# Moving two kinds of store from ScalarE's DMA queue to SyncE's in a one-core attention and mixture-of-experts kernel

## The chip, the core and the metric

The kernel runs on one core of a Trainium2 chip. The number that counts is the device time of one execution in microseconds (us). Five engines work in parallel, each through its own instruction stream in a fixed order: TensorE (PE, with its weight loads PEld), VectorE (DVE), ScalarE (ACT), GpSimd (POOL) and SyncE (SP), which only starts transfers (DMA). ACT and POOL can start transfers too; in the profile these issues stand as SPq, ACTq and POOLq. Engines wait for each other and for transfers through semaphores.

## What is computed

Sixteen sequences of 512 rows by 256 columns go through one layer: attention with 16 heads of 16 columns, rotary positions and a linear position bias, then a residual and a layer norm; then a shared feed-forward part plus the best two of eight experts for each row, then again residual and norm. Cut to what matters:

```
qkv = x @ qkv_w.T;  q, k = rotary(q), rotary(k)
w = softmax(q @ k.T * SCALE + min(j - i, 0) * slope * 8)
x = layernorm(x + (w @ v) @ proj_w.T + proj_b)
shared = silu(x @ sW1 + sb1) @ sW2 + sb2
top_vals, top_idx = top_k(sqrt(softplus(x @ routing_W.T + bias)), 2)
y_e = silu(x @ rW1[e] + rb1[e]) @ rW2[e] + rb2[e]
x = layernorm(x + shared + sum over the two experts of top_val * y_e)
```

## The kernel before

**Steps.** All engines run the same loop over steps `s` (from -36 to 711), and a table of numbers says in which step each job of each sequence falls. A sequence takes 32 steps of attention (steps 0 to 511 for the sixteen), in four groups of eight; its later jobs follow at fixed distances. A step is no barrier: it only fixes the order inside each engine's stream. Semaphores do the rest, so an engine can be ahead of another or behind it.

**Attention, seen from SP.** In every eight steps, for one group of four heads, SP does the following in this order: it writes row maxima to memory (`m_out`, L452) and reads them back into the operand `qa` (`m_rows_in`, four transfers at L459); it writes the sums of the softmax (`sums_out`, L464), waits until they have landed and reads them back in another shape (`sums_in`, L470); it loads the next group's operands (`assemble`, six transfers at L390 and L393, four at L429 and L430); it writes the reciprocals (`rec_out`, L474), waits for the landing and spreads them (`rec_rows`, four at L484). Beside these it writes projected queries and keys (`parts_out`, L422).

**Sparse experts.** Fourteen of the sequences go through a sorted layout: their rows are scattered to memory by expert, in three groups of 6, 6 and 2 sequences, and are then worked off in blocks of 256 rows, 31, 31 and 15 of them (77). `BLOCKS_AT` gives their steps: in the first group mostly one block in four steps, in the second one in two, in the third one in each step. For a block, SP reads two table entries into registers (L499, L500) and loads the rows `xg` (L503), the weights `wb` (L507) and a bias (L510), two steps ahead of its first use or, where blocks are dense, one; PE turns the rows (L802), multiplies by the first weights (L810) and the second (L818, L820); ACT copies the result to `yb[q % 3]` (`down_block`, L1472), three steps after the turn; and one step later the copy is stored to `d_y` (`store_block`, L1479) from ACT's stream, just behind that step's two exponentials (L1368). ACT's copy of block q + 3 waits until that store has landed.

**Finals.** When a group's blocks are stored, POOL gathers each row's two expert results (L1602), DVE adds them to the base (L1192, L1194), which SP has loaded into `bs[b % 2]` (`base_in`, L527, which waits on the landing of the result that was in that buffer, L526), POOL computes the scale, and ACT normalizes in place (`norm2`, four at L1420, step offset `NORM2` = 8). One step later ACT's stream stores the result to `out` (L1532, offset `OUT` = 9).

**Dense experts.** The last two sequences go through all eight experts. SP loads each expert's weights (`load_expert`, L520 and L521); the buffers are four, and a load waits until the expert four earlier is through. PE multiplies at L832 and L845.

Of the kernel before, what the change touches and what calls it, by code (L numbers as in the profile page):

```python
# [67 lines left out]
LOADB, TURNB, UPB, GATEB, DOWNB, STOREB = (-2, 0, 1, 2, 3, 4)  # L68
# [9 lines left out]
DENSE_AT = ((93, 1), (86, 1))  # L78
LOADD, GATED, DOWND = (-5, 1, 2)
WEIGHTS, VAR3, NORM3, OUTD = (0, 24, 25, 27)  # L80
BASE_IN, GATHER, ADD, VAR2, NORM2, OUT = (-1, (1, 2, 2, 4), (3, 4, 5, 6), 6, 8, 9)
LATE, PREP, PADS = 11, (18, 20, 22, 24), 40

WARM = (5, 6, 4, 4, 5)
# [6 lines left out]
ROWS = 256  # L91
# [5 lines left out]
FIRST_BLOCK = [sum(NBLOCKS[:g]) for g in range(len(GROUPS) + 1)]  # L97
# [43 lines left out]
def block_due(s, at):  # L141

    return BLOCK_OF.get(s - at, -1)


def final_due(s, at):

    return FINAL_OF.get(s - at, -1)
# [32 lines left out]
def _build(nc, ctx, A, out):  # L181
# [95 lines left out]
    yb = [sb(f"yb{i}", [128, 2, C]) for i in range(3)]  # L277
# [4 lines left out]
    bs = [sb(f"bs{i}", [128, 4, C]) for i in range(2)]  # L282
# [44 lines left out]
    out_w = [sem(f"out_w{i}") for i in range(2)]  # L327
# [38 lines left out]
    def bk(job, i, b):  # L366

        return G[(job, i), b][0]

    def full(job, i, b):  # L370

        return G[(job, i), b][1] + 1
# [25 lines left out]
    def _(e):  # L398
# [93 lines left out]
        def load_block(q):  # L492
            g = GROUP_OF_BLOCK[q]
            j = q - FIRST_BLOCK[g]
            if j == 0:
                e.wait_ge(s_tab, g + 1)
                e.wait_ge(rows_w, 16 * 8 * (LAST_OF[g] + 1))
                e.wait_ge(pad_w, 32)
            row = e.value_load(tab[0:1, g, j:j + 1], min_val=0, max_val=E * REGION - ROWS)  # L499
            wrow = e.value_load(tab[0:1, g, JMAX + j:JMAX + j + 1], min_val=0, max_val=(E - 1) * 128)  # L500
            if q >= NX:
                e.wait_ge(g_full[bk("turnb", 0, q - NX)], full("turnb", 0, q - NX))
            e.dma_start(xg[q % NX][:, :, :], d_x[g % 2][bass.ds(row, ROWS), :].rearrange("(p k) c -> p k c", k=2)  # L503
                        ).then_inc(xg_in[q % NX], 16)
            if q > 3:
                e.wait_ge(g_full[bk("downb", 0, q - 4)], full("downb", 0, q - 4))
            e.dma_start(wb[q % 4][:, :], A["wb"][bass.ds(wrow, 128), :]).then_inc(wb_in[q % 4], 16)  # L507
            if q == 0:
                e.wait_ge(rb_w, 32)
            e.dma_start(rb2[q % 4][0:2, :], d_rb[bass.ds(wrow, 2), :]).then_inc(wb_in[q % 4], 16)  # L510

        def load_expert(n):
# [7 lines left out]
            e.dma_start(wbd[n % 4], A["wb"][x * 128:x * 128 + 128, 0:512]).then_inc(wbd_in[n % 4], 16)  # L520
            e.dma_start(rbd[n % 4][0:2, :], d_rb[x * 128:x * 128 + 2, :]).then_inc(wbd_in[n % 4], 16)  # L521

        def base_in(b):
            e.wait_ge(base_w, 16 * (b + 1))
            if b > 1:
                e.wait_ge(out_w[b % 2], 16 * (b // 2))  # L526
            e.dma_start(bs[b % 2][:, :, :], d_base[b].rearrange("(t p) c -> p t c", p=128)).then_inc(bs_in[b % 2], 16)  # L527
# [14 lines left out]
        for s in range(FIRST, LAST):  # L542
            if (g := (s - M_OUT) // 8 - 1) >= 0 and (s - M_OUT) % 8 == 0 and g < 4 * NB:
                m_out(g)
            if (g := (s - M_IN) // 8 - 1) >= 0 and (s - M_IN) % 8 == 0 and g < 4 * NB:
                m_rows_in(g)
            for g in range(4):
                if (b := due(s, EVAC + SUMS_OUT + 8 * g)) >= 0:
                    sums_out(4 * b + g)
                if (b := due(s, EVAC + SUMS_IN + 8 * g)) >= 0:  # L550
                    sums_in(4 * b + g)
                if (b := due(s, EVAC + REC_OUT + 8 * g)) >= 0:
                    rec_out(4 * b + g)
                if (b := due(s, EVAC + REC_IN + 8 * g)) >= 0:
                    rec_rows(4 * b + g)
            if s == 3:
                load_xT(1)
            if s == LATE:
                e.dma_start(idf[:, :], A["k_idf"]).then_inc(l_id, 16)
                load_x(0)  # L560
                e.dma_start(wp[:, :, :], A["wp"]).then_inc(l_w, 16)
                e.dma_start(pb[:, :], A["pb"].rearrange("(a c) -> a c", a=1).broadcast_to([128, C])).then_inc(l_w, 16)
                e.dma_start(w1[:, :, :], A["w1"]).then_inc(l_w, 16)
                e.dma_start(w2[:, :], A["w2"]).then_inc(l_w, 16)
                e.dma_start(rw[:, :, :], A["rwT"]).then_inc(l_w, 16)
                e.dma_start(b1[:, :], A["b1"]).then_inc(l_w, 16)
                e.dma_start(bias2[0][E:E + 1, :], A["sb2"].rearrange("(a c) -> a c", a=1)).then_inc(l_w, 16)
                for t in range(4):
                    e.dma_start(ebb[:, t, :], A["eb"].rearrange("(a c) -> a c", a=1).broadcast_to([128, E])).then_inc(l_w, 16)
                e.dma_start(bias2[0][0:E, :], A["rb2"]).then_inc(l_w, 16)  # L570
                e.dma_start(wkey[:, :, :], A["k_key"]).then_inc(l_w, 16)
                e.dma_start(before[:, :, :], A["k_before"]).then_inc(l_w, 16)
                e.dma_start(run0[:, :], A["k_run"]).then_inc(l_w, 16)
                e.dma_start(tk[:, :], A["k_tk"]).then_inc(l_w, 16)
                e.dma_start(th[:, 0:128], A["k_on2"]).then_inc(l_w, 16)
                e.dma_start(bd[:, :], A["b1s"]).then_inc(l_bd, 16)
            if s == PREP[3]:
                e.wait_ge(s_rb, 2)
                e.wait_ge(s_zero, 1)
                for k in range(2):  # L580
                    e.dma_start(d_rb.rearrange("(x r) c -> r x c", r=128)[k], bias2[1 + k]).then_inc(rb_w, 16)
                e.wait_ge(rb_w, 32)
                e.dma_start(sb2[0:2, :], d_rb[E * 128:E * 128 + 2, :]).then_inc(rb_in, 16)
            if s == PADS:
                for i in range(2):
                    e.dma_start(d_x[i].rearrange("(x r) c -> r x c", x=E)[0:ROWS],
                                A["x"][0, 0:ROWS].rearrange("r (x c) -> r x c", x=1).broadcast_to([ROWS, E, C])
                                ).then_inc(pad_w, 16)
            for q in LOAD_BLOCKS.get(s, ()):
                load_block(q)  # L590
            for i in range(4):
                if (b := due(s, QK[i][-1] + SHUFFLE[i] + PARTS_OUT)) >= 0:
                    parts_out(b, i)
                    if 4 * b + i == 1:
                        e.wait_ge(p_k0, 16)
                        key_rows(0)
            if (g := (s - ASSEMBLE) // 8) >= 0 and (s - ASSEMBLE) % 8 == 0 and g < 4 * NB:
                assemble(g)
            if (b := due(s, XT_LOAD)) > 1:
                load_xT(b)  # L600
            if (b := due(s, X_LOAD)) > 0:
                load_x(b)
            if 0 <= (b := due(s, BASE_OUT)) < SPARSE:
                base_out(b)
            for n in LOAD_EXPERTS.get(s, ()):
                load_expert(n)
            if (k := last_due(s, OUTD)) >= 0:
                e.wait_ge(s_od, k + 1)
                e.dma_start(out[SPARSE + k].rearrange("(t p) c -> p t c", p=128), x1[(SPARSE + k) % 2][:, :, :]
                            ).then_inc(out_d, 16)  # L610
            if (b := final_due(s, BASE_IN)) >= 0:
                base_in(b)
        for i in range(2):
            e.wait_ge(out_w[i], 16 * ((SPARSE + 1 - i) // 2))
        e.wait_ge(out_d, 16 * DENSE)
# [741 lines left out]
    def _(e):  # L1357
# [114 lines left out]
            e.mul(yb[q % 3][:, :, :].rearrange("p k c -> p (k c)"), pG[bk("downb", 0, q)][:, :], 0.5  # L1472
                  ).then_inc(g_free[bk("downb", 0, q)], 1)

        def store_block(q):
            g = GROUP_OF_BLOCK[q]
            j = q - FIRST_BLOCK[g]
            e.wait_ge(g_free[bk("downb", 0, q)], full("downb", 0, q))
            e.dma_start(d_y[g][j * ROWS:(j + 1) * ROWS, :].rearrange("(p k) c -> p k c", k=2), yb[q % 3][:, :, :]  # L1479
                        ).then_inc(y_w[q % 3], 16)  # L1480

        e.dma_start(sl[:, :], A["slopes"].rearrange("(a h) -> a h", a=1).broadcast_to([128, H])).then_inc(l_sl, 16)
        e.dma_start(hot, A["k_hot"]).then_inc(l_pos, 16)
        e.dma_start(bpos[0:32], A["k_pos"][0:32]).then_inc(l_pos, 16)
# [4 lines left out]
        for s in range(FIRST, LAST):  # L1489
            if 0 <= s - LAG < NC:  # L1490
                exps(s - LAG)
            if (q := block_due(s, STOREB)) >= 0:
                store_block(q)
            for g in range(4):
                if (b := due(s, EVAC + 8 * g)) >= 0:
                    evacuate(4 * b + g)
# [30 lines left out]
                e.activation(sp[:, 2, 0:8 * ALL_GROUPS[g]], sp[:, 1, 0:8 * ALL_GROUPS[g]], ACT.Exp).then_inc(s_u, 1)  # L1527
            if (b := final_due(s, NORM2)) >= 0:
                norm2(b)
            if (b := final_due(s, OUT)) >= 0:  # L1530
                e.wait_ge(s_o, b + 1)
                e.dma_start(out[b].rearrange("(t p) c -> p t c", p=128), bs[b % 2][:, :, :]).then_inc(out_w[b % 2], 16)  # L1532
            if (b := due(s, UP[1])) >= 0:
                up(b)
            if (n := dense_due(s, 0)) >= 0:
# [192 lines left out]
```

## Time and profile before

| What | us |
|---|---|
| median of three runs | 1660.75 |
| the three runs | 1657.20, 1660.75, 1663.59 |
| the profiled execution, its own time | 1663.59 |
| its span in the trace | 1661.8 |
| transfers' mean rate from 1300 to 1400 | 206 GB/s |

PE is busy for 88% of the span, DVE 71%, ACT 61%, POOL 44%. ACT's figure counts its computing instructions; register, semaphore and DMA-issuing instructions of an engine are not counted as busy, so SP has no figure at all although its stream has some two thousand instructions. What SP does is seen in the timeline, in the list of what it waited for, and in the chain: the work that ended last, followed back from the end, at each step to what released it. SPq in that chain is time in which nothing but SP's issuing stood between one event and the next.

### The profile page before, as it was taken

The page shows a single profiled execution, that of the slowest core. Times are in us where ns is not written, and L with a number is a line of the kernel's source. Part 1 is how long each engine was busy: PE and PEld are TensorE (multiplying, and loading weights), DVE is VectorE, ACT ScalarE, POOL GpSimd, SP SyncE. Part 2 cuts the span into 40 slices and gives each one's busy share as a digit, 9 for nine tenths or more (in the row PEclk, how much of TensorE's full clock was granted, in tenths as well). Part 3 has the DMA queues.
Part 4 walks back from the last instruction along what each step waited for, and adds up shares of the span by engine and source line. Part 5 has one row for each costly group of instructions (what it writes and reads, how often), then busy time and mean ns, then how long its engine had stood idle before and what let it go on. Part 6 is the DMA issues. An engine that isn't in the chain of part 4 may idle for free.

```text
span 1661.8 us, 33130 instructions
## 1 busy us (share of the span) xinstructions
PE 1458.4 (88%) x11110; PEld 801.2 (48%) x11110; DVE 1171.7 (71%) x2631; ACT 1019.3 (61%) x1742; POOL 723.9 (44%) x655
## 2 busy tenths in 40 slices
PE   7987999999999889899999899988888999896467
PEld 4433444444444435555555544454455555564345
DVE  7665777878778787666666677857776577645674
ACT  1465666666767656666677576666566587675242
POOL 2233353635545343541535253533666344255630
PEclk8789899999999989999999999999999899998789
DMA  7334243434343324454545433443566566686531
GB/s 208 115 109 147 91 124 101 129 108 132 102 123 116 115 92 141 132 175 139 178 138 165 130 120 116 128 139 120 166 214 222 177 217 209 192 257 212 168 106 51
DMA packets 185349, 242.00 MB, mean 146 GB/s; under 512 B 67239, under 2 KB 104190, under 8 KB 185182
## 3 DMA queue, kind: packets, MB, share of 16 engines
q1 hardware_dynamic: 154746, 181.18, 36.4%
q0 software_dynamic: 10752, 29.37, 5.4%
q10 hardware_dynamic: 19684, 29.33, 5.0%
q8 instruction: 91, 1.49, 0.4%
q14 instruction: 76, 0.62, 0.1%
HBM read 152.53 MB, written 91.44 MB: 147 GB/s over the span
## 4 chain that ended last, share of the span: by engine, by line
PE 51%; DVE 15%; SPq 14%; DMA 10%; issue 6%; POOL 2%; ACT 2%; POOLq 0%; ACTq 0%; DVEq 0%
PE pS L641 15%; PE pV L683 9%; PE pG L707 6%; DVE negm L932 5%; PE pG L729 3%; PE pG L716 3%; SPq L390 2%; DMA xg<-d_x 2%; PE pS L647 2%; DMA d_rec<-scr 2%; PE pG L810 2%; SPq L459 2%; PE pG L818 2%; SPq L499 1%; DMA d_sum<-pvs 1%
## 5 line engine op out<-in xcount | busy, mean ns | idle before, releaser
L932 DVE TENSOR_REDUCE negm<-pS 128x1 f32<-128x512 f32 x1024 | 659.6, 683 | 336.4 <-PE pS L647 329.6
L1368 ACT ACTIVATE ee<-pT,slp 128x512 f32<-128x512 f32 x1024 | 649.0, 684 | 216.8 <-PE pT L668 215.2
L641 PE MATMUL pS<-ka,qa 62*128 62x512 f32 x1024 | 485.4, 509 | 81.0 <-DVE negm L932 68.3
L662 PE MATMUL pT<-qa,ka 64*128 64x512 f32 x1024 | 480.9, 504 | 0.2 <-ACT ee L1368 0.2
L641 PEld LDWEIGHTS pS<-ka,qa 62*128 62x128 f32 x1024 | 198.4, 194 | 330.0 <-issue 312.8
L683 PE MATMUL pV<-ee,vv 128*32 128x512 f32 (+1 forms) x2048 | 286.8, 633 | 0.0
L647 PE MATMUL pS<-mAB,tri 64*128 64x64 bf16 x2048 | 243.6, 200 | 0.0
L668 PE MATMUL pT<-mAB,tri 64*128 64x64 bf16 x2048 | 239.9, 198 | 0.0
L1555 POOL TENSOR_TENSOR raw<-raw,rope 128x512 f32<-128x512 f32 x61 | 78.2, 1282 | 330.0 <-DVE sh L966 329.9
L662 PEld LDWEIGHTS pT<-qa,ka 64*128 64x128 f32 x1024 | 195.6, 191 | 4.5 <-issue 3.1
L647 PEld LDWEIGHTS pS<-mAB,tri 64*128 64x128 bf16 x2048 | 119.8, 99 | 139.6 <-issue 107.3
L1575 POOL TENSOR_TENSOR rs<-ve,minus 128x4 f32<-128x4 f32 x32 | 34.1, 1067 | 280.3 <-DVE ve L1014 280.3
L707 PE MATMUL pG<-xT,wqkv 128*128 128x512 f32 x256 | 149.6, 670 | 4.6 <-DVE wqkv L1274 2.4
L1602 POOL DMA_INDIRECT gg<-d_y,posy x112 | 111.5, 995 | 60.1 <-issue 29.0
L1590 POOL DMA_INDIRECT d_x<-x,pos x112 | 115.3, 1030 | 48.0 <-issue 24.6
L668 PEld LDWEIGHTS pT<-mAB,tri 64*128 64x128 bf16 x2048 | 118.0, 97 | 28.2 <-issue 24.8
L1609 POOL TENSOR_TENSOR pvs<-pvs 128x512 f32<-128x512 f32 x32 | 40.7, 1271 | 172.8 <-DVE pvs L956 172.8
L729 PE MATMUL pG<-wp,pvs 128*128 128x256 f32 x256 | 70.3, 409 | 28.9 <-POOL pvs L1609 28.9
L818 PE MATMUL pG<-wb,zbb 128*128 128x256 f32 x308 | 93.6, 397 | 1.0 <-DVE zbb L1182 1.0
L1384 ACT COPY raw<-pG 128x512 f32<-128x512 f32 x63 | 36.9, 586 | 85.6 <-PE pG L707 68.3
L810 PE MATMUL pG<-xgT,wb 128*128 128x256 f32 x308 | 84.1, 397 | 4.0 <-DVE x L1178 3.2
L1456 ACT COPY xgT<-pG 128x512 f32<-128x512 f32 x77 | 44.8, 582 | 66.4 <-PE pG L802 66.4
(186 smaller groups left out, 2192.8 us busy)
## 6 DMA issues: line engine op xcount, KB each, us to landing
d_part<-parts SPq DMA_DIRECT2D x63, 512.0 KB, 2.8
qa<-d_part SPq DMA_DIRECT2D x378, 64.0 KB
wb<-in_wb SPq DMA_DIRECT2D x77, 256.5 KB
xg<-d_x SPq DMA_DIRECT2D x77, 256.0 KB, 2.9
d_y<-yb ACTq DMA_DIRECT2D x77, 256.0 KB, 2.6
ka<-d_part SPq DMA_DIRECT2D x128, 128.0 KB
xT<-in_xT SPq DMA_DIRECT2D x16, 512.0 KB
ka<-d_part SPq DMA_DIRECT2D x128, 64.0 KB
```

The source lines that it names most:

```text
L641: e.matmul(pS[:, k, :], qa[g % 4][r, i, t * 128:t * 128 + 128].bitcast(F32R), ka[g % 4][r, i, :].bitcast(F32R), start=True, stop=False)
L647: last = e.matmul(pS[:, k, c0:c0 + 64], tri[r, a, :], mAB[r, 1, i, :], start=False, stop=(a == 1))
L662: e.matmul(pT[:, k, :], ka[g % 4][r, i, kt * 128:kt * 128 + 128].bitcast(F32R), qa[g % 4][r, i, :].bitcast(F32R), start=True, stop=False)
L668: last = e.matmul(pT[:, k, c0:c0 + 64], tri[r, 2 + a, :], mAB[r, 0, i, :], start=False, stop=(a == 1))
L683: last = e.matmul(pV[32 * hh:32 * hh + m, :], vv[b % 2][:, 17 * kt + r0:17 * kt + r0 + m, h], ee[:, k, (4 * w + 2 * (hh % 2) + hh // 2) % ...
L707: last = e.matmul(pG[bk("qk", i, b)][:, :], wqkv[:, c, col:col + 128], xT[b % 2][:, c, :], start=(c == 0), stop=(c == 1))
L729: last = e.matmul(pG[bk("proj", j, b)][:, t * C:(t + 1) * C], pvs[:, (4 * b + 2 * p) % SETS, (2 * j + t) * 128:(2 * j + t + 1) * 128], wp[ ...
L810: last = e.matmul(p[:, 0:ROWS], wb[q % 4][:, c * 128:c * 128 + 128], xgT[q % 2][:, c, :], start=(c == 0), stop=(c == 1))
L818: e.matmul(p[:, k * C:(k + 1) * C], zbb[q % 2][:, k * 128:k * 128 + 128], wb[q % 4][:, 256:512], start=True, stop=False)
L932: e.tensor_reduce(negm[:, g % 2, j, t + k:t + k + 1], pS[:, k, :], AX, ALU.max, negate=True).then_inc(s_max, 1)
L1368: e.activation(ee[:, k, d % 7, :], pT[:, k, :], ACT.Exp, scale=slp[:, 6, h:h + 1]).then_inc(s_exp, 1)
L1590: e.indirect_dma_start(d_x[g % 2], bass.IndirectOffsetOnAxis(pos[:, b % 2, n, t:t + 1], 0), x1[b % 2][:, t, :], None).then_inc(rows_w, 16)
```

## The change

`store_block` and the store of the normalized result move from ACT's stream to SP's. In a step, SP now issues the block's store behind the loads of blocks that fall in that step and ahead of `parts_out` and `assemble`; the result's store is the last thing of its step. Each brings its wait along: the store of a block waits on ACT's copy, that of a result on `norm2`. `OUT` goes from 9 to 8, so that the result's store stands in the step of `norm2` itself.

```diff
-BASE_IN, GATHER, ADD, VAR2, NORM2, OUT = (-1, (1, 2, 2, 4), (3, 4, 5, 6), 6, 8, 9)
+BASE_IN, GATHER, ADD, VAR2, NORM2, OUT = (-1, (1, 2, 2, 4), (3, 4, 5, 6), 6, 8, 8)
@@ SP's stream
+        def store_block(q):
+            g = GROUP_OF_BLOCK[q]
+            j = q - FIRST_BLOCK[g]
+            e.wait_ge(g_free[bk("downb", 0, q)], full("downb", 0, q))
+            e.dma_start(d_y[g][j * ROWS:(j + 1) * ROWS, :].rearrange("(p k) c -> p k c", k=2), yb[q % 3][:, :, :]
+                        ).then_inc(y_w[q % 3], 16)
...
             for q in LOAD_BLOCKS.get(s, ()):
                 load_block(q)
+            if (q := block_due(s, STOREB)) >= 0:
+                store_block(q)
...
             if (b := final_due(s, BASE_IN)) >= 0:
                 base_in(b)
+            if (b := final_due(s, OUT)) >= 0:
+                e.wait_ge(s_o, b + 1)
+                e.dma_start(out[b].rearrange("(t p) c -> p t c", p=128), bs[b % 2][:, :, :]).then_inc(out_w[b % 2], 16)
@@ ACT's stream: store_block is gone, and with it
-            if (q := block_due(s, STOREB)) >= 0:
-                store_block(q)
...
-            if (b := final_due(s, OUT)) >= 0:
-                e.wait_ge(s_o, b + 1)
-                e.dma_start(out[b].rearrange("(t p) c -> p t c", p=128), bs[b % 2][:, :, :]).then_inc(out_w[b % 2], 16)
```

In the order of the instructions, SP's stream gets 91 transfers more (77 blocks, 14 results). Two places matter.

The first is SP in the second group of blocks, in one eight-step round; the difference shows both kinds of store around `rec_out`. `d_rec` holds the reciprocals, `rb_0` is a block's bias, `yb` its result, `bs` a normalized sequence; line numbers behind the change are seven or more higher for the same code.

```order
 L510 ISA
 L510 DMA rb_0<-d_rb 2x256
-L474 DMA d_rec<-scr 128x16 [waits s_rec]
+L527 DMA d_y<-yb 128x512 [waits g_free0]
+L474 DMA d_rec<-scr 128x16 [waits s_rec]
+L624 DMA out<-bs 128x4x256 [waits s_o]
 L484 DMA rb<-d_rec 16x512 [waits s_att,rec_w1]
 L484 DMA rb<-d_rec 16x512 x3
```

A block's store now stands between the last load of the block and the next thing of the round, here `rec_out`; the result's store stands between `rec_out` and the wait for its landing.

The second is SP near the end, where `rope` and `wqkv` are reused as buffers for the dense experts' weights and `parts` for their biases. Before:

```order
L521 DMA parts<-d_rb 2x256
L527 DMA bs<-d_base 128x4x256 [waits out_w1,base_w]
L520 DMA rope<-in_wb 128x512 [waits s_yd]
L521 DMA parts<-d_rb 2x256
L520 DMA rope<-in_wb 128x512 [waits s_yd]
```

Now:

```order
L521 DMA parts<-d_rb 2x256
L534 DMA bs<-d_base 128x4x256 [waits out_w1,base_w]
L624 DMA out<-bs 128x4x256 [waits s_o] x2
L520 DMA rope<-in_wb 128x512 [waits s_yd]
L521 DMA parts<-d_rb 2x256
```

The stores of the last two sparse sequences, with their waits on `norm2`, now stand ahead of the weight loads of the last sequence's first four experts.

## Rows read from the trace of the kernel before

**Rows 1.** The page, part 4: the chain by engine.

```profile
PE 51%; DVE 15%; SPq 14%; DMA 10%; issue 6%; POOL 2%; ACT 2%; POOLq 0%; ACTq 0%; DVEq 0%
```

**Rows 2.** What PE waited for, 640 to 1515: total, times, longest.

```profile
PE pG L802 <- DMA xg<-d_x: 38.7, 21, 4.0
...
```

**Rows 3.** What SP waited for, 1214.2 to 1276.7: total, times, longest.

```profile
SPq L484 <- DMA d_rec<-scr: 7.0, 2, 3.7
SPq L470 <- DMA d_sum<-pvs: 2.7, 2, 1.6
```

**Rows 4.** The same, 1341.4 to 1403.3.

```profile
SPq L470 <- DMA d_sum<-pvs: 5.2, 2, 2.9
SPq L484 <- DMA d_rec<-scr: 4.5, 2, 2.7
```

**Rows 5.** The same, 1276.8 to 1341.4.

```profile
...
SPq L474 <- DVE scr L952: 4.5, 1, 4.5
...
```

**Rows 6.** SP's first table load per block, 1203.6 to 1283.4 and 1329.7 to 1414.1.

```profile
L499 SPq TENSOR_LOAD <-tab x11: 451/473/1201, 1203.7 to 1281.6; - x11
...
L499 SPq TENSOR_LOAD <-tab x11: 453/474/967, 1331.6 to 1412.5; - x11
```

**Rows 7.** The chain where the first stretch ends: start, length, what.

```profile
1283.36 2.87 DMA xg<-d_x
...
```

**Rows 8.** The chain on SP, 1273: start, length, what.

```profile
1273.11 0.29 SPq L510
...
1273.51 0.35 SPq L422
...
1273.91 0.73 SPq L459
```

**Rows 9.** Timeline of ACT, 1236: start, length, engine, line, operation.

```profile
1236.25 0.67 ACT L1368 ACTIVATE ee<-pT,slp 128x512 f32<-128x512 f32 x1
1236.36 0.33 ACTq L1479 DMA_DIRECT2D d_y<-yb  x1
1236.82 0.68 ACT L1368 ACTIVATE ee<-pT,slp 128x512 f32<-128x512 f32 x1
...
1239.74 1.26 ACT L1368 ACTIVATE ee<-pT,slp 128x512 f32<-128x512 f32 x2
```

**Rows 10.** The moved stores, all: issue in ns min/median/max; landing in us.

```profile
L1479 ACTq DMA_DIRECT2D d_y<-yb x77: 326/326/355, 643.6 to 1521.7; - x77
...
DMA to landing us min/median/max: 2.0/2.6/6.0
...
L1532 ACTq DMA_DIRECT2D out<-bs x14: 378/396/462, 1203.2 to 1610.4; - x14
```

**Rows 11.** ACT's first store and SP's bias load at the same place of the order.

```profile
L1479 ACTq DMA_DIRECT2D d_y<-yb x11: 326/326/333, 1206.1 to 1282.6; - x11
...
1210.30 0.29 SPq L510 DMA_DIRECT2D rb<-d_rb  x1
```

**Rows 12.** What SP waited for, 831.9 to 855.2.

```profile
...
SPq L474 <- DVE scr L952: 0.9, 1, 0.9
...
```

**Rows 13.** What SP waited for, 1444 to 1503.

```profile
...
SPq L474 <- DVE scr L952: 1.9, 2, 1.2
...
SPq L507 <- PE pG L820: 1.3, 1, 1.3
```

**Rows 14.** A window near the end: busy PE, PEld, DVE, ACT, POOL; clock, DMA share, GB/s.

```profile
1614.70:1620.40 5.70, 5.69 (x11) 3.27 (x12) 2.27 (x10) 2.07 (x4) 2.53 (x3) 0.50 0.00 0
```

**Rows 15.** Timelines near the end, of SP, PE and ACT.

```profile
1587.62 0.33 SPq L520 DMA_DIRECT2D rope<-in_wb  x1
...
1600.67 1.88 PE L832 MATMUL pG<-x1T,rope 128*128 128x512 f32 x4
1614.71 1.19 PE L791 MATMUL pG<-w,hs 128*128 128x256 f32 x2 [12.17 <-DVE hs L1164]
...
1610.40 0.38 ACTq L1532 DMA_DIRECT2D out<-bs  x1
```

More of the change, by code:

```diff
@@ L1473, in down_block @@
                   ).then_inc(g_free[bk("downb", 0, q)], 1)
[L1475 to L1480, printed above, removed]
         e.dma_start(sl[:, :], A["slopes"].rearrange("(a h) -> a h", a=1).broadcast_to([128, H])).then_inc(l_sl, 16)
```

## The prediction, made before the run

> **What bounds the kernel now.** I read the chain of waits first. It runs on PE for half the span, but 14% of it is SP's issuing and 10% are transfers, and ACT's issuing has 0% [rows 1]. Then what PE waits for while blocks are worked off, from 640 to 1515: most often and longest for the block rows `xg` that SP loads, 38.7 us in 21 waits, more than for DVE [rows 2]. Then what SP itself waits for. From 1214 to 1277 and from 1341 to 1403 it waits for nothing but the landing of its own two small round trips, the sums and the reciprocals [rows 3, 4]; there is no wait for an engine. There SP is the bottleneck: whatever is put into its stream pushes back all that stands behind it. The chain says the same: it lies on SP and on SP's transfers without a break from the table load at 1203.7 to the load that lands for PE behind 1283.36, and again from about 1330, just ahead of the table load at 1331.6, to the load that follows the last table load at 1412.5 [rows 6, 7]. Between the two SP does wait for DVE, 4.5 us [rows 5]. In the first group of blocks it is less tight: in the round from 831.9 to 855.2 its longest engine wait is 0.9 us [rows 12]. In the third group, 1444 to 1503, they are 1.9 and 1.3 us in two and a half rounds [rows 13].
>
> **What ACT gets back: about nothing.** A block's store sits behind the first exponential of its step. At 1236.36 it is issued in 0.33 us while that exponential is still running (1236.25 to 1236.92), and the second begins 0.57 us behind the first; of the two from 1239.74, with no store between, the second begins 1.26 - 0.69 = 0.57 us behind the first as well [rows 9]. So 77 times 0.33 us [rows 10] are hidden under ACT's arithmetic, and taking them away saves 0. One result store near the end is not hidden: at 1610.40 it stands 0.38 us between the last `norm2` and an exponential for which DVE waits [rows 15]. Gain: 0.4 us.
>
> **What SP pays.** The nearest row is `parts_out`, one transfer with one wait. The bias load ends at 1273.40, `parts_out` is issued in 0.35 us, and the next transfer starts at 1273.91 [rows 8]: 0.51 us in all, of which some 0.07 would stand there as a gap anyway. I take 0.44 for a block's store, and 0.48 for a result's, whose issue is 0.07 longer on ACT (0.396 to 0.326) [rows 10]; all together 77 × 0.44 + 14 × 0.48 = 40.6 us of SP's time. From below the cost is 0, where SP would have waited anyway; from above it is these 40.6. Does the new wait on ACT's copy block SP? No: SP lags. Counting through the new order, the second group's first store within the stretch falls behind the bias load that ends at 1210.6, and ACT had issued that store at 1206.1 [rows 11]. Laid on each other in this way, the two streams show SP at the place of the store mostly 2 to 14 us after the copy is finished. So the stores go out late but without waiting. Late stores hold ACT's copy three blocks on; in the third group, one block per step, I find 2 us or more between the landing (2.6 us) and that copy, so this costs nothing in the forecast.
>
> Group by group:
> - Second group, the two stretches on SP: 11 loads in each [rows 6]. The first load has a result's store behind it and no block's, the last load ends the stretch. That leaves 9 and 10 block stores and 4 result stores, of which one stands between `rec_out` and the wait for its landing and is hidden. 19 × 0.44 + 3 × 0.48 = 9.8 us, all on the path.
> - Between the stretches: 6 block stores and a result, 3.1 us, against 4.5 us of waiting for DVE [rows 5], some of which come behind a late load. I take 1.0; from 1414 to 1444, 0.5 of four stores' 1.8.
> - Third group, 13 block and 2 result stores until 1503: 6.7 us against 3.2 us of engine waits [rows 13]. 2.5 us, between 0 and 6.7.
> - First group, 31 stores, two in a round, 0.88 us a round. PE waits for `xg` in about every second round. There the store ahead of `assemble` counts, and often that behind `rec_rows`: 8 rounds × 0.66 = 5.3, and 0.2 for the others; 5.5, between 0 and 31 × 0.44 = 13.6. The round in rows 12 has 0.9 us of slack for its 0.88, which is why I don't take more.
> - The end: the weight load for the last sequence's first expert is issued at 1587.62 and used by PE at 1600.67, in time that PE has to spare [rows 15]. Now it stands behind two result stores, the second of which waits for the `norm2` that ends at 1610.37. Issues at 1610.45 and 1610.9, landing about 2.9 us later (the time of a block's rows, of the same size [rows 7]): 1613.8. PE then starts 0.9 us sooner than its 1614.71, but with the four products that it had done before, 1.88 us at the higher clock. PE had idled for 12.17 us [rows 15], and its granted clock was 0.50, the lower level (1.2 GHz), from 1614.7 to 1620.4 [rows 14]. If that stretch starts at 1613.8 and is as long, 3.6 us of it go to these products, 2.1 to the next, and the dense stage starts 0.6 us later. Bounds: -0.4 if the load lands sooner, +3.5 if it takes the 6.0 us of the slowest block store [rows 10]. With the 0.4 of ACT: +0.2 us.
> - In the tail before that, SP is held by a result's store ahead of the last reciprocals' rows. They arrive a little later, while POOL is still busy with gathers: 0.
>
> Sum: 9.8 + 1.0 + 0.5 + 2.5 + 5.5 + 0.2 = 19.5 us on the profiled execution's 1663.6, which is 1683.1. The median of the runs is 2.8 us below that execution, so I forecast 1680.3, rounded to 1680; from the bounds of its terms this case reaches from 1670 to 1691.
>
> The Trainium skill ("DMA: Bandwidth & Descriptors", section "Issuing engines are not separate DMA queues") says that transfers started by different engines run on the same DMA engines, and that spreading them saves only the sequencer's time to issue, usually small beside the transfer. Beside the landing of 2.6 us the 0.33 us is small indeed [rows 10]; but by that rule the sequencer's time is all that this change gives up, and it gives it up on the one that has none to spare.
>
> **Rivals.**
> - *Absorbed.* SP's round has waits on landings; if the loads that become late are ones for which PE has slack in more rounds than I think, only the two bound stretches count, and of them perhaps half: about 5 us, 1666. For it: 4.5 us of slack lie between the stretches [rows 5]. Against it: no engine wait at all inside them [rows 3, 4]. Chance 0.17.
> - *Queued behind the store.* Now 256 KB of a block's store go ahead of the reciprocals' small transfer on SP's own queue, and SP stands still until that has landed. At the mean rate from 1300 to 1400, 206 GB/s, 256 KB are 1.3 us; in eight rounds of the second and third group that adds 10 us: 1691. For it: that landing cost 3.7 us where loads stood just ahead [rows 3]. Against it: the same bytes passed the same engines before. Chance 0.16. The Trainium skill ("DMA: Bandwidth & Descriptors", section "Queues, rings and completion order") has each DMA engine take one queue's descriptors in ring order and alternate between queues by packets. By that rule the small transfer would overtake a store on ACT's queue but not one on SP's, which speaks for this rival; no row of before can show it.
> - *SP seizes up.* A late store holds ACT's copy in the third group, PE waits for ACT, and the weights for the last experts land late (+3.5): 15 blocks × 0.7 us more, 1680 + 10.5 + 3.3 = 1694. The 2 us of room speak against it. Chance 0.07.
> - *Faster.* ACT's issues were not hidden, and their 77 × 0.33 + 14 × 0.40 = 31.0 us come off the path: 1660.75 - 31.0 + 19.5 = 1649. It wins from the point where more than 19.5 of the 31.0 us stood on the path. ACT has 2% of the chain and its issuing 0% [rows 1], and rows 9 show one overlapped. Chance 0.05.
>
> **How the numbers follow.** Forecast 0.55, then 0.17, 0.16, 0.07 and 0.05. What a measurement can tell from no change is about 0.5%, 8.3 us: up to 1669.1 counts as the same. Slower: 0.55 + 0.16 + 0.07, less 0.01 for the low edge of my own case, 0.77. Same: 0.17. With the 0.01 and part of the faster case that stays small, 0.18. Faster: 0.05. The range of 8 in 10 reaches from 1663, which holds most of the absorbed case, to 1697, which takes in the landings' case and the stall.
>
> **What would show it.** Right: in the second group SP's engine waits near 0, PE's waits for `xg` longer in sum than 38.7 by some 10 to 20 us; block issues of 0.35 us on SP with no wait before them; exponentials still 0.57 us apart on ACT, so ACT's busy time unchanged and its idle time larger; PE's first product of the last sequence at about 1614 plus the shift. The landings' rival would show as longer waits of L484 on `d_rec`. I am wrong if PE's waits for `xg` don't grow, if SP's new stores wait for ACT's copies, or if the stretches around 1203 to 1283 and 1330 to 1414 keep their length.

## The result and the profile after

| | median us | runs | ratio to before, 95% interval |
|---|---|---|---|
| before, same chip | 1661.93 (1657.2 to 1663.59) | 4 | |
| changed | 1680.96 (1677.53 to 1693.48) | 4 | 1.0133 [1.0097, 1.0168] |

The change costs 1.33%, 22.1 us by the ratio, with an interval of 16 to 28 us; between the two medians lie 19.0. 1680 was forecast, and slower. The record holds nine more runs of the changed kernel, from 1678.16 to 1695.45 us; the median of all thirteen is 1683.03. The profiled execution of the changed kernel is the slowest of them, 1695.45 us, 14.5 above the median in the table, so what it shows of sizes by stage is too large by that much in all; the sizes below are taken from ratios. In the changed kernel the block's store is L527 and the result's L624; lines of SP between them are 7 higher, those of PE, DVE and ACT mostly 12 higher. In the tables of this document two of e8's six runs (4198.71 and 7189.06 us) and one run of the kernel before beside e4, e5, e6 and e8 (2142.97 us) were in a slow state and count in no ratio.

The page's chain by engine, which answers to [rows 1]:

```profile
PE 44%; SPq 21%; DVE 13%; DMA 11%; issue 7%; another core or an unknown queue 1%; POOL 1%; ACT 1%; POOLq 0%; DVEq 0%; ACTq 0%
```

SP's issuing has 21% of the chain, where it had 14%. What PE waited for from 640 to 1530, against [rows 2] (total, times, longest):

```profile
PE pG L814 <- DMA xg<-d_x: 50.6, 23, 5.9
...
```

PE's waits for SP's loads grew by 11.9 us, as the prediction asked for. The moved stores on SP, against [rows 10] (issue in ns: min/median/max):

```profile
L527 SPq DMA_DIRECT2D d_y<-yb x77: 3/353/1452, 645.8 to 1552.6; - x77
...
L624 SPq DMA_DIRECT2D out<-bs x14: 378/416/562, 1211.9 to 1640.8; - x14
```

What SP waited for in the two stretches that answer to [rows 3] and [rows 4], from 1220.0 to 1292.9 and from 1360.5 to 1424.8:

```profile
SPq L484 <- DMA d_rec<-scr: 4.6, 1, 4.6
SPq L470 <- DMA d_sum<-pvs: 2.6, 2, 1.5
SPq L390 <- PE pT L680: 0.4, 1, 0.4
```

```profile
SPq L470 <- DMA d_sum<-pvs: 3.6, 2, 2.5
SPq L484 <- DMA d_rec<-scr: 2.0, 1, 2.0
```

Still no wait of SP for an engine but 0.4 us; it never waits there for ACT's copy. In the whole run the list has 0.9 us of that wait, once.

The list's waits for the reciprocals' landing (L484) look shorter than before, 4.6 and 2.0 us after 7.0 and 4.5, but it names one wait in each stretch where SP makes two such round trips. SP's timeline has them all; in the first stretch:

```profile
1236.49 0.42 SPq L474 DMA_DIRECT2D d_rec<-scr  x1
1241.71 1.72 SPq L484 DMA_DIRECT2D rb<-d_rec  x4
...
1273.04 0.46 SPq L474 DMA_DIRECT2D d_rec<-scr  x1
1276.47 1.72 SPq L484 DMA_DIRECT2D rb<-d_rec  x4
```

From the issue of `rec_out` to that of its rows pass 5.22 and 3.43 us here, 3.05 and 3.95 in the second stretch, 15.7 in all. The same four trips take 3.64, 4.22, 2.28 and 3.12 before, 13.3 in all. With 256 KB of a block's store just ahead of each of them in SP's own ring they are longer by 0.6 us each on average, in one execution. Whether that comes from the bytes is taken up with e3.

A row of SP's timeline (start, length, engine, line) shows a store in its place, between the bias load and the query rows, 0.47 us from its start to that of the next transfer:

```profile
1259.76 0.29 SPq L510 DMA_DIRECT2D rb<-d_rb  x1
1260.10 0.35 SPq L527 DMA_DIRECT2D d_y<-yb  x1
1260.57 1.26 SPq L390 DMA_DIRECT2D qa<-d_part  x2
```

On ACT, against [rows 9], a pair of exponentials that had the store behind its first:

```profile
1253.93 1.25 ACT L1380 ACTIVATE ee<-pT,slp 128x512 f32<-128x512 f32 x2
```

1.25 us for two of 0.68, so the second begins 0.57 us behind the first, as with the store between them. ACT got nothing back there, and its busy time over the whole run is 1021.4 us after 1019.3.

### The profile page after: what moved, and what is told of

Read it like the earlier page. It is cut to its first block, busy times and chain, and to the rows that moved or that the text cites. A ratio compares the mean times of both kernels' runs of the same rounds, so it can differ in the third digit from the quotient of the medians.

```text
span 1693.6 us, 33130 instructions
## 1 busy us (share of the span) xinstructions
PE 1470.3 (87%) x11110; PEld 807.4 (48%) x11110; DVE 1169.2 (69%) x2631; ACT 1021.4 (60%) x1742; POOL 723.3 (43%) x655
## 4 chain that ended last, share of the span: by engine, by line
PE 44%; SPq 21%; DVE 13%; DMA 11%; issue 7%; another core or an unknown queue 1%; POOL 1%; ACT 1%; POOLq 0%; DVEq 0%; ACTq 0%
PE pS L653 13%; PE pV L695 8%; DVE negm L944 5%; PE pG L719 5%; SPq L390 3%; SPq L459 3%; DMA xg<-d_x 3%; PE pG L728 3%; DMA d_rec<-scr 2%; PE pG L741 2%; PE pS L659 2%; SPq L499 2%; SPq L393 2%; SPq L484 2%; SPq L430 1%
## 5 line engine op out<-in xcount | busy, mean ns | idle before, releaser
L1609 POOL TENSOR_TENSOR pvs<-pvs 128x512 f32<-128x512 f32 x32 | 40.7, 1273 | 177.1 <-DVE pvs L968 177.1
L814 PE MATMUL pG<-idf,xg 128*128 128x128 f32 x308 | 50.2, 287 | 51.5 <-DMA xg<-d_x 50.6
```

## The experiments

Each ratio is to runs of the kernel before on the same chip, taken beside those of the experiment. That kernel's median was 1663.76 us beside the first four experiments of the table, 1675.14 beside the next four, 1660.75 and 1673.55 beside the last two pairs, so plain times of different groups are not compared; a difference in us is the ratio's excess times that median.

| experiment | ratio, 95% interval | us |
|---|---|---|
| e1: only the block stores on SP | 1.0115 [1.0070, 1.0161] | +19.1 |
| e2: only the result stores on SP | 1.0034 [1.0005, 1.0063] | +5.7 |
| e3: 77 small transfers added on SP | 1.0124 [1.0077, 1.0171] | +20.6 |
| e7: changed, block stores in SP's waits | 1.0012 [0.9983, 1.0042] | +2.0 |
| e4: 154 small transfers added on SP | 1.0257 [1.0203, 1.0311] | +43.1 |
| e5: before, key rows' loads on ACT | 0.9848 [0.9795, 0.9901] | -25.5 |
| e6: changed, key rows' loads on ACT | 0.9928 [0.9901, 0.9955] | -12.1 |
| e8: e7 and key rows' loads on ACT | 0.9860 [0.9798, 0.9921] | -23.5 |
| e9: block stores of the first group on SP | 1.0031 [1.0009, 1.0052] | +5.1 |
| e10: block stores of the later groups on SP | 1.0077 [1.0049, 1.0104] | +12.8 |
| e11: 77 small transfers added on ACT | 0.9996 [0.9970, 1.0021] | -0.7 |
| e12: e2 with `norm2` a step earlier | 1.0023 [0.9994, 1.0053] | +3.8 |

### Which stores cost: blocks alone, results alone

e1 is the change without L624 and with `OUT` left at 9; e2 is the change without L527, its block stores on ACT as before.

> Only the 77 block stores are on SP; the 14 result stores stay on ACT at offset 9. Theory (SP's issue time on the path): the 19.5 us of the forecast less the three result stores in the bound stretches (1.4) and the late weight load at the end (0.6, with the 0.4 us of ACT not regained): about 17 us over before, 1679. Rival (the result stores, whose wait on norm2 blocks SP, carry the loss): at most 5 us over before, 1667.

> Only the 14 result stores are on SP, at offset 8; the block stores stay on ACT. Theory: 3 x 0.48 us in the bound stretches and 0.2 at the end, about 2 us over before, 1664, which is near what can't be told from no change. Rival (result stores carry the loss): 12 us or more over before, 1674.

The blocks cost 19.1 us, as the theory had it. The results cost 5.7, more than the 2 expected, though the interval reaches from 0.8 to 10.5. The trace of e2, an execution 13.3 us above its median, suggests a cause that the forecast had ruled out for block stores and taken over for results without a count. What SP waited for in e2 from 1282.5 to 1320.7:

```profile
SPq L470 <- DMA d_sum<-pvs: 5.2, 1, 5.2
SPq L615 <- ACT bs L1423: 3.9, 1, 3.9
...
```

SP stands at the result's store 3.9 us for ACT's `norm2`, with all its loads behind it, and 2.3 us in the next such round: where SP is not held up by 77 block stores it reaches these waits early enough to stand in them.

e12 puts `norm2` where SP no longer meets it; against e2:

```diff
-BASE_IN, GATHER, ADD, VAR2, NORM2, OUT = (-1, (1, 2, 2, 4), (3, 4, 5, 6), 6, 8, 8)
+BASE_IN, GATHER, ADD, VAR2, NORM2, OUT = (-1, (1, 2, 2, 4), (3, 4, 5, 6), 6, 7, 8)
```

> Only the result stores on SP, as in the kernel that cost 5.6 us instead of the 2 expected, but with ACT's norm2, on which each store waits, one step earlier (step 7 of the sequence's last phase instead of 8), so that it is over before SP comes to the store. Theory (of the 5.6 us some 6 were SP's waits of 3.9 and 2.3 us for norm2 within the second group): these waits go, ratio 1.000 to 1.002. Rival (the price is the 14 issues or where the stores land): ratio 1.003 to 1.005 as before. Where norm2 in its new place waits for DVE and holds ACT, the time rises though the waits go, and the pair decides nothing.

The two waits are gone from the second group in its trace, and the ratio is 1.0023, between what the two sides expected and with an interval that holds both. Whether the waits or the 14 issues make up the price of the results alone stays open.

### Issue time or bytes

e3 leaves all stores on ACT and adds, at each place where the change issues a block's store, a transfer of 4 KB with the same wait; e4 adds two.

```diff
+        def tiny(q):
+            e.wait_ge(g_free[bk("downb", 0, q)], full("downb", 0, q))
...
+            e.dma_start(d_small[q], idf[:, 0:8]).then_inc(small_w, 16)
...
+            if (q := block_due(s, STOREB)) >= 0:
+                tiny(q)
```

> The kernel before, with its block stores on ACT, and in addition at each of the 77 places where the changed kernel has a block store on SP a transfer of 4 KB over 128 partitions (instead of 256 KB) with the same wait; its data are not used. It costs SP the same issue but puts no bytes into its queue. Theory (issue time): the same loss as with the block stores alone, about 17 us over before, 1679. Rival (the bytes that go ahead of SP's small transfers in its own queue): at most 7 us over before, 1669.

> The kernel before, with two extra transfers of 4 KB on SP at each place where the change issues a block store (154 in all, one wait per place as before). With one extra transfer per place the time rose from 1663.8 to 1684.3, 20.6 us or 0.27 us for each of 77. Theory (SP's issue time is what costs, and it adds up): the second transfer costs at least as much as the first, +40 to +50 us, 1704 to 1714. Rival (the first transfer costs only by its place or by its wait on ACT's copy, the work that follows is free): not above 1690, as with one. Rival (SP has slack in part of the program, so that more load makes further rounds bound): the second costs more than the first, above 1714.

4 KB cost 20.6 us, 256 KB cost 19.1 (e1): the bytes do not carry the loss, and the rival by which e3 costs at most 7 us has fallen, since its interval begins at 12.8. Nor do the bytes show in the four round trips of the reciprocals above: by the timelines they take 17.8 us in e1 and 17.4 in e3, and 14.8 in e11, where SP's stream is that of before (13.3). An effect of the bytes of a few us in all is not excluded: e1 and e3 each have an interval of some 15 us. Two transfers cost 43.1 us, within the 40 to 50 expected: 2.1 times one, 0.28 us for each of 154. The added ones on SP in e4 (issue in ns, min/median/max):

```profile
L529 SPq DMA_DIRECT2D d_small<-idf x77: 12/353/643, 649.4 to 1566.6; - x77
L530 SPq DMA_DIRECT2D d_small<-idf x77: 3/432/1895, 649.8 to 1567.0; - x77
```

### The same transfers on ACT

e11 adds the same 77 transfers of 4 KB behind ACT's block stores, without a wait of their own.

```diff
             if (q := block_due(s, STOREB)) >= 0:
                 store_block(q)
+                tiny(q)
```

> The kernel before, with 77 extra transfers of 4 KB issued by ACT, each right behind a block store (so two issues stand behind the first exponential of the step). The same 77 on SP cost 20.6 us. Theory (ACT's issues are hidden under the exponential in front of them): ratio 0.998 to 1.003, and the second exponential still starts about 0.57 us behind the first. Rival (the second issue sticks out of the 0.67 us of the exponential): up to 77 x 0.1 us on ACT, which costs where ACT is waited for: ratio 1.003 to 1.006. Rival (an issue costs the same wherever it stands): ratio 1.012.

No cost: -0.7 us, within 0.3% either way. ACT's timeline in e11:

```profile
1238.01 0.67 ACT L1371 ACTIVATE ee<-pT,slp 128x512 f32<-128x512 f32 x1
1238.03 0.33 ACTq L1482 DMA_DIRECT2D d_y<-yb  x1
1238.39 0.45 ACTq L1488 DMA_DIRECT2D d_small<-idf  x1
1238.58 0.68 ACT L1371 ACTIVATE ee<-pT,slp 128x512 f32<-128x512 f32 x1
```

Two issues, 0.78 us together, begin under the first exponential, and the second exponential still starts 0.57 us behind it. The second issue even runs on beneath the second exponential, which no row of before had shown. The same transfer costs 0.27 us on SP and nothing here.

### The stores in SP's idle time

e7 is the changed kernel with the block stores until step 503 moved, on SP, to behind `sums_out` and ahead of the wait of `rec_rows`, where SP is going to stand anyway until a small transfer lands.

```diff
+        def flush(s):
+            while pending:
+                store_block(pending.pop(0))
+            if hidden(s) and (q := block_due(s, STOREB)) >= 0:
+                store_block(q)
...
                     sums_out(4 * b + g)
+                    flush(s)
...
                 if (b := due(s, EVAC + REC_IN + 8 * g)) >= 0:
+                    flush(s)
                     rec_rows(4 * b + g)
```

> The changed kernel, but until step 503 the block stores stand where SP waits for a landing anyway: between the writing of the sums and the wait for them, and just ahead of the wait for the reciprocals, two in each at most. Stores of the third group (15) stay where the change put them. Theory (issue time counts where it isn't covered): 0.88 us in a landing wait of 1.1 us or more is covered; what is left is the third group, the result stores and the end, 3 to 8 us over before, 1665 to 1670. Rival (the number of SP's instructions counts wherever they stand, or late stores hold ACT): no better than the changed kernel, 1681 or more.

Of the change's 22.1 us 2.0 are left, between -2.8 and 7.0, with every store still on SP; 3 to 8 were expected. SP's timeline in e7, two stores issued behind `rec_out` (L474), ahead of the rows that wait for its landing:

```profile
1256.49 0.34 SPq L474 DMA_DIRECT2D d_rec<-scr  x1
1256.88 0.93 SPq L527 DMA_DIRECT2D d_y<-yb  x2
1259.27 1.74 SPq L484 DMA_DIRECT2D rb<-d_rec  x4
```

From `rec_out`'s start to the rows' start pass 2.78 us, two stores included. Without a store in it this round trip takes from 2.3 to 4.2 us in the two stretches of before: the stores fit in. From 1180 to 1450 SP's waits for the two landings fell to:

```profile
SPq L484 <- DMA d_rec<-scr: 12.5, 7, 3.9
SPq L470 <- DMA d_sum<-pvs: 5.1, 6, 2.5
```

17.6 us; the list leaves out two trips of each kind, and by the timeline SP stood idle in all of them for some 22 us. In the kernel before they were 37.0 over the same window, by the list and by the timeline:

```profile
SPq L484 <- DMA d_rec<-scr: 19.1, 9, 3.7
SPq L470 <- DMA d_sum<-pvs: 17.9, 9, 3.8
```

The stores have filled what was waiting.

### Taking load off SP

e5 is the kernel before with the four loads of a group's key rows (L429, L430), for groups from the fifth on, issued by ACT behind exponentials, two each in two steps.

```diff
+    def key_half(e, g, c):
...
+        e.dma_start(ka[g % 4][r0:r0 + 32, :, :], k_[c::2].rearrange("a d p t -> (d p) a t")).then_inc(qk_in[g % 4], 16)
+        e.dma_start(ka[g % 4][r0 + 32:r0 + 48, :, :], k_[c::2, :, 0, :].rearrange("a d t -> d a t")
+                    ).then_inc(qk_in[g % 4], 16)
...
-            if g:
+            if 0 < g < 4:
                 key_rows(g)
```

e6 is the same edit on the changed kernel, e8 on e7.

> The kernel before, stores left on ACT, and for every group from the fifth on the four transfers that load its key rows (lines L429 and L430) are issued by ACT behind two of its exponentials instead of by SP. SP loses some 1.7 us of issue in each of 60 rounds of 8 steps. Theory (SP bounds the rounds, ACT's issues are hidden under its exponentials): the kernel gets faster than before by a part of that, since PE's own floor is near once SP is relieved: 1635 to 1655. Rival (SP does not bound the rounds; a store on SP costs by when it lands): 1660 to 1668, no change. Rival (ACT cannot issue for nothing): slower than 1668.

> The changed kernel (block and result stores on SP) with the same move of the key rows to ACT. SP gains 91 issues of 0.35 to 0.45 us and loses about 240. Theory (SP bounds, and what it carries is what counts, not which transfer): most of the 17 to 19 us of the change go away, 1645 to 1668, and against the kernel with only the key rows moved the stores cost less than the 17 us that they cost here, 5 to 12 us. Rival (a store on SP costs by itself, by its bytes or by its place in SP's ring): the stores cost the same 17 us on top of the kernel with only the key rows moved.

> The changed kernel with both edits: the block stores until step 503 issued inside SP's waits for a landing, and the key rows of groups 5 to 64 issued by ACT. Each removes load from the stretches in which SP has no slack. Theory: within 3 us of the kernel before with only the key rows moved, 1638 to 1658, and the fastest with the stores on SP. Rival (the placement in SP's waits has gained all that the relief of SP can give): the same as with the placement alone, 1662 to 1667.

e5 is 25.5 us faster than before, 0.11 us for each of the 240 transfers moved. Its chain, PE's waits for `xg` from 640 to 1515, and SP's longest wait over the whole run:

```profile
PE 64%; DVE 14%; issue 5%; DMA 5%; SPq 5%; ACT 3%; POOL 2%; another core or an unknown queue 1%; ACTq 1%; POOLq 0%; DVEq 0%
```

```profile
...
PE pG L813 <- DMA xg<-d_x: 11.9, 9, 2.9
```

```profile
SPq L485 <- DVE scr L963: 180.3, 50, 12.5
```

SP's issuing falls from 14% of the chain to 5%, PE's waits for `xg` from 38.7 us [rows 2] to 11.9, and SP now stands 180.3 us for DVE's reciprocals, where over the whole run of before this wait was 79.7:

```profile
SPq L474 <- DVE scr L952: 79.7, 36, 10.5
```

So SP has slack. In e6 the changed kernel's stores cost on top of e5 1.0081, 13.4 us: less than the 22 of the change and more than the 5 to 12 expected. With the intervals of both, 13.4 lies between some 4 and 23 us, so it is told apart neither from 5 to 12 nor from 17 or 22: that the stores cost less once SP is relieved is not shown by the times. e6's chain has SP's issuing at 9%, and PE's waits for `xg` from 640 to 1515 are:

```profile
PE pG L825 <- DMA xg<-d_x: 16.8, 13, 3.6
```

With the stores in SP's waits as well, e8 is 2 us above e5, as expected, but its ratio rests on four runs and the difference is known to some 13 us only. The lowest ratio is e5's, with the stores where they were: 0.9848, 1.5% below before.

### Where in the program the cost arises

e9 has the block stores of the first group on SP (`q < 31` on SP, the others on ACT), e10 those of the second and third.

```diff
+            if (q := block_due(s, STOREB)) >= 0 and q < 31:
+                store_block(q)
```

> The kernel before, in which only the 31 block stores of the first group (those from 643 to 1163 us) are issued by SP, at the place of the change; the other 46 block stores and the result stores stay on ACT. In the forecast this term was 5.5 us, between 0 and 13.6. By the shift between the two profiled executions it was about 6.5 us. Theory (the cost is shared among the groups as SP's slack is): ratio about 1.0035, 5 to 8 us. Rival (all of the cost of the block stores comes from the stretches with no slack at all, behind 1200): 0 to 2 us.

> The kernel before, in which only the 46 block stores behind 1200 us are issued by SP. In the forecast the second and third group's block stores were 19 x 0.44 + 0.9 + 0.5 + 2.2, about 12 us. Theory: ratio about 1.007, 10 to 14 us, and with the kernel that has only the first group's on SP it adds up to the 19 us of all 77. Rival (these stores were under-priced by the forecast, as the shift of some 25 us behind 1200 between the two profiled executions says): 17 us or more.

5.1 and 12.8 us, 17.9 together, against 19.1 for all 77 in e1: the parts add up. The times at which SP issues the sums at four places, e9 and then e10:

```profile
632.76 0.55 SPq L464 DMA_DIRECT2D d_sum<-pvs  x1
...
1181.95 0.54 SPq L464 DMA_DIRECT2D d_sum<-pvs  x1
...
1433.49 0.55 SPq L464 DMA_DIRECT2D d_sum<-pvs  x1
...
1531.42 0.53 SPq L464 DMA_DIRECT2D d_sum<-pvs  x1
```

```profile
630.87 0.55 SPq L464 DMA_DIRECT2D d_sum<-pvs  x1
...
1179.59 0.54 SPq L464 DMA_DIRECT2D d_sum<-pvs  x1
...
1443.25 0.55 SPq L464 DMA_DIRECT2D d_sum<-pvs  x1
...
1542.52 0.54 SPq L464 DMA_DIRECT2D d_sum<-pvs  x1
```

The same marks of the kernel before, and the middle two of the changed kernel:

```profile
633.60 0.55 SPq L464 DMA_DIRECT2D d_sum<-pvs  x1
...
1179.02 0.54 SPq L464 DMA_DIRECT2D d_sum<-pvs  x1
...
1432.84 0.55 SPq L464 DMA_DIRECT2D d_sum<-pvs  x1
...
1526.48 0.53 SPq L464 DMA_DIRECT2D d_sum<-pvs  x1
```

```profile
1182.64 0.54 SPq L464 DMA_DIRECT2D d_sum<-pvs  x1
...
1457.54 0.54 SPq L464 DMA_DIRECT2D d_sum<-pvs  x1
```

Lengths of the three stages between the marks: before 545.4, 253.8, 93.6; e9 549.2, 251.5, 97.9; e10 548.7, 263.7, 99.3; changed 552.7, 274.9, 99.3. The changed kernel's second stage, which holds both bound stretches, is 21.1 us longer, in an execution 14.5 us above the median: the stretches did not keep their length, which was a sign of being wrong. e9's first stage grows by 3.8 and its second does not grow; e10's second grows by 9.8. But e9's third grows by 4.3 with nothing on SP there, and in e11, whose time is that of before, the second is 5.3 and the third 7.9 longer. A stage's length in one execution moves by that much by itself, so it hints at places, and the sizes come from the ratios.

## Why the prediction was right

**ACT gets back nothing: shown.** Exponentials 0.57 us apart without the store, ACT's issuing 0% of the chain before and after, and e11, where 77 more issues on ACT cost -0.7 us.

**SP pays by its issue time: shown.** Taken was 0.44 us per block store on a path without slack; over all 77, slack included, it is 0.25 (e1). e3 and e4 give the same answer without moving a store: +20.6 and +43.1. The bytes do not carry the cost (e3 against e1), and the cost goes when the same issues stand in SP's waits (e7).

**SP lags, so the stores don't wait for ACT's copy: right in the changed kernel for blocks.** The two stretches show no such wait. For the results it was right in the second group, with one wait of 0.9 us; alone (e2) they wait 3.9 and 2.3 us there. That the block stores hold SP back long enough in the changed kernel is the likely reason, not a tested one. Behind 1560 SP does stand at result stores, 37.8 us in four waits for `norm2`, the longest 13.4. The prediction named that hold and priced it at nothing; what the whole end costs is told below.

**The terms.** First group: 5.5 forecast, 5.1 measured (e9, 1.5 to 8.6). The block stores of the later groups: of the forecast's 9.8 + 1.0 + 0.5 + 2.5, the results' 3 x 0.48 = 1.4 and a share of the 2.5 are not theirs, which leaves about 12; measured 12.8 (e10, 8.1 to 17.3). All blocks: about 17.5 forecast, 19.1 measured (e1). Results: about 2 forecast, 5.7 alone (e2), and 22.1 - 19.1 = 3.0 on top of the blocks. By the middle values this is the term that was sized too low, and it, with one or two us of the blocks, makes the difference of 19.5 to 22.1; but both differences lie within the intervals. That the median came out at 1680.96 against 1680 is luck: intervals of 5 us and more stand on each term, the median of all thirteen runs is 1683.03, and the forecast took 2.8 us off for a profiled execution above its median.

**The end.** Forecast: PE starts 0.9 us before its old start in the last sequence's expert, with four products it had done before, at the lower clock in 3.6 us. PE's timeline there (start, length; in brackets the idle time before), and the window behind it (busy PE, PEld, DVE, ACT, POOL, then clock, DMA share, GB/s), against [rows 14, 15]:

```profile
1634.50 3.23 PE L790 MATMUL pG<-x1T,w 128*128 128x512 f32 x4
1644.93 3.75 PE L844 MATMUL pG<-x1T,rope 128*128 128x512 f32 x4 [7.20 <-issue]
```

```profile
1644.90:1651.00 6.10, 6.07 (x11) 3.56 (x12) 0.80 (x6) 2.25 (x5) 2.18 (x3) 0.52 0.28 91
```

The four products moved behind the idle time, which is 7.20 us where it was 12.17. The shift up to there is 30.4 us, by the last mark below and by the end of the last `norm2` (1640.77 after 1610.37). PE starts at 1644.93, 0.2 us before its old start so shifted (1614.71 + 30.4 = 1645.1), where 0.9 was forecast: from the issue of the weights to PE's start pass 3.7 us, not 2.9. The products took 3.75 us at a granted clock of 0.52, the lower level, where 3.6 was forecast; SP issues their weights at 1641.22, right behind the last result's store:

```profile
1640.80 0.38 SPq L624 DMA_DIRECT2D out<-bs  x1
1641.22 0.51 SPq L520 DMA_DIRECT2D rope<-in_wb  x1
```

The last mark, 1556.87, stands 30.4 us behind that of before, and the whole span is 31.8 longer: 1.4 us for all that lies behind it, in one execution, against 0.2 forecast. It is no more than such a difference moves by itself. One thing differs there that was not forecast: ACT and with it PE stand for more than 4 us at about 1629 for something that the profile doesn't name, and the four products ahead of the idle time take 3.23 us where they took 1.94. It fell into time that PE had to spare.

**The rivals.** *Queued behind the store* asked for 1.3 us in each of eight rounds. It fell: the four trips measured grew by 0.6 each, in e3 with 4 KB ahead they are as long as in e1 with 256, and e3 costs as much as e1. *Absorbed* (5 us) fell with the result's lower bound of 16 us. *Faster* fell with e11. *SP seizes up* asked for 10.5 us in the third group and 3.3 at the end; with 10.5 more e10 would have cost some 22 us, and its interval ends at 17.3. The Trainium skill ("DMA: Bandwidth & Descriptors", section "Issuing engines are not separate DMA queues") was quoted for the sequencer's time being what spreading saves. The runs agree: e3's 20.6 us for 4 KB transfers and e1's 19.1 for 256 KB have that time in common and not the bytes. "Usually small" is said of an issue beside its transfer, 0.33 us beside 2.6 here, and holds; for an engine that has no slack it is no measure of the price, which for 77 such issues is 1.2% of this kernel.

## What to carry to other kernels

Look in the chain for the queue whose issuing has a share of it, and at what that engine waits for: if only for landings of its own transfers, each further transfer there costs up to its whole issue time (0.3 to 0.45 us here, 0.27 on average over the 77 places of e3), at 4 KB as at 256, and each taken away gives some back until the next engine is late. Count the waits in the timeline, since the list of waits can leave some out. An engine with long instructions of its own (here ACT's exponentials of 0.67 us) could issue for nothing beneath them. If a transfer must stand on the full queue, put it between the start of a round trip and the wait for its landing.

## What had not been expected of the hardware

- Two issues in a row on ACT, 0.33 and 0.45 us, hid beneath two exponentials without moving either (e11).
- SP has spots where issues stand 1.4 us apart with records of almost no length. The changed kernel's profiled execution has one in the second group:

```profile
1280.32 0.35 SPq L503 DMA_DIRECT2D xg<-d_x  x1
1281.73 0.00 SPq L507 DMA_DIRECT2D wb<-in_wb  x1
1283.15 0.00 SPq L510 DMA_DIRECT2D rb<-d_rb  x1
1283.16 0.02 SPq L527 DMA_DIRECT2D d_y<-yb  x1
```

  Three transfers that elsewhere take some 1.4 us in all take 2.8. What SP did there no run shows. From 560 us on, between 16 and 25 such records stand in the profiled executions of the changed kernel, e4, e5, e6, e8, e11 and e12, and none in those of before, e1, e2, e3, e7, e9 and e10. e11's has 20 of them and took its kernel's median time, so they do not by themselves explain an execution above the median.
- The kernel before had medians from 1660.75 to 1675.14 us beside the different experiments, 0.9% apart, and these two on the same chip: a change of 1% can only be read against runs of before taken beside it.
